# Seven half products instead of eight (Strassen) for the gate and up products of the expert stage

## What is computed

```
scores = softmax(x @ gate_w.T)                     # 64 experts, the best 8 are kept in w_e
flat = w_e[:, inv_map]                             # (tokens, 8 groups, 8)
soft = softmax(where(flat == 0, -1e9, flat))
xg = x[:, None, :] + einsum('ngi,ghi->ngh', soft, mask_up_w)
g = einsum('ngh,gih->ngi', xg, gate_proj_w)
u = einsum('ngh,gih->ngi', xg, up_proj_w)
d = einsum('ngi,ghi->ngh', silu(g) * u, down_proj_w)
y = einsum('ng,ngh->nh', flat.sum(-1), d)
out = layernorm(x + y)
```

## Time and profile before

| | us |
|---|---|
| median of 3 runs | 2915.49 (2913.86 to 2915.83) |
| the profiled execution | 2915.24 |
| its span, first to last instruction | 2913.5 |
| PE busy in it | 2688.2 (92%) |
| DVE, ACT, POOL busy | 1899.0, 1596.0, 1313.3 |

### The profile page before, as it was taken

The page is one execution under the profiler, slowest core; times in us unless marked ns, Lnnn a source line. Parts: engine busy times, 40 slices in busy tenths (PEclk is TensorE's granted clock), DMA queues, the critical chain, the costliest instruction groups (busy, mean ns, idle before and its releaser), DMA issues. The chain is left out here.

```text
span 2913.5 us, 48708 instructions
## 1 busy us (share of the span) xinstructions
PE 2688.2 (92%) x16876; PEld 1534.9 (53%) x16876; DVE 1899.0 (65%) x3477; ACT 1596.0 (55%) x3668; POOL 1313.3 (45%) x1326
## 2 busy tenths in 40 slices
PE   6789886899999999869987999999899999999998
PEld 4667672455555555534435666666554444444443
DVE  5778897887787787677746788886473333332335
ACT  7999993665656656644427777776442222222121
POOL 3889895877676766324325111111042222222121
PEclk8999998999999999989997999999989999999999
DMA  5112113322221222420011000000032211111201
GB/s 166 39 55 77 43 40 84 94 44 41 44 39 37 44 40 60 141 71 1 1 46 49 19 20 14 15 20 19 9 101 69 68 31 69 65 67 31 69 33 69
DMA packets 154010, 148.99 MB, mean 51 GB/s; under 512 B 108721, under 2 KB 113201, under 8 KB 152402
## 3 DMA queue, kind: packets, MB, share of 16 engines
q1 hardware_dynamic: 153810, 146.49, 17.7%
HBM read 112.57 MB, written 4.52 MB: 40 GB/s over the span
## 5 line engine op out<-in xcount | busy, mean ns | idle before, releaser
L2233 POOL TENSOR_TENSOR s_state<-s_state,s_ct 128x512 f32<-128x512 f32 x256 | 326.6, 1301 | 81.0 <-DVE s_state L2408 78.6
L891 POOL TENSOR_TENSOR m_aTl<-m_prod,m_aTh 128x512 bf16<-128x512 f32 x88 | 101.6, 1155 | 559.7 <-ACT m_aTh L965 559.7
L2408 DVE TENSOR_TENSOR_SCAN s_state<-s_decay,s_psd 128x512 f32<-128x512 f32 x256 | 301.7, 1209 | 67.3 <-PE s_psd L2553 33.3
L1150 DVE TENSOR_TENSOR m_prod<-m_bank,m_gated 128x512 f32<-128x512 f32 x88 | 60.9, 692 | 406.3 <-ACT m_gated L963 406.3
L963 ACT ACTIVATE m_gated<-m_bank 128x512 f32<-128x512 f32 x88 | 52.5, 596 | 403.0 <-PE m_bank L1281 220.4
L1264 PE MATMUL m_bank<-m_xTh,m_wh 128*128 128x512 bf16 x704 | 267.4, 380 | 2.0 <-DVE m_prod L1150 1.2
L1265 PE MATMUL m_bank<-m_xTl,m_wh 128*128 128x512 bf16 x704 | 267.2, 380 | 0.0
L2553 PE MATMUL s_psd<-ident,s_v 128*128 128x128 f32 x1024 | 164.7, 286 | 43.0 <-DVE s_state L2408 22.0
L2309 ACT ACTIVATE s_decay<-s_dt,s_nega 128x508 f32<-128x508 f32 x256 | 181.6, 710 | 19.3 <-DVE s_state L2408 19.2
L2322 ACT ACTIVATE s_v<-s_uT,s_bT 128x512 f32<-128x512 f32 x256 | 182.1, 712 | 1.1 <-PE s_psd L2553 1.0
L2553 PEld LDWEIGHTS s_psd<-ident,s_v 128*128 128x128 f32 x1024 | 121.8, 146 | 90.0 <-ACT s_v L2322 47.9
(11 more groups left out here) (511 smaller groups left out, 7866.9 us busy)
## 6 DMA issues: line engine op xcount, KB each, us to landing
s_ct<-ssm_bc SPq DMA_DIRECT2D x64, 256.0 KB, 3.0
m_scale<-moe_scale SPq DMA_DIRECT2D x64, 256.0 KB, 3.1
m_stage<-in_moe_w_dram SPq DMA_DIRECT2D x16, 768.0 KB, 4.6
m_stage<-in_moe_w_dram SPq DMA_DIRECT2D x8, 1024.0 KB, 8.5
X<-in_x_dram SPq DMA_DIRECT2D x4, 1024.0 KB, 11.1
staging<-in_xa_wq_dram SPq DMA_DIRECT2D x8, 512.0 KB, 4.1
a_cf<-in_ctxT_dram SPq DMA_DIRECT2D x16, 256.0 KB, 2.9
staging<-in_xa_wo_dram SPq DMA_DIRECT2D x8, 512.0 KB, 4.4
```

What stands on the lines that cost most here:

```text
L2233: pool.tensor_tensor(h, h, ct[t % 4][:, s * P:(s + 1) * P].unsqueeze(1).broadcast_to([P, KB, P]), ALU.mult).then_inc(weighted, 1)
L2408: dve.tensor_tensor_scan(state[i % RING][:, :], decay[t % 2][:, s, :, :].rearrange("p m t -> p (m t)"), ps_d[i % 2][:, :], 0.0, ALU.mult, ...
```

## The change

In sections 1 to 7 a block's gate and up are made together. The tokens of a quarter are two halves of 256 (`TH`), the 512 inputs two halves, and gate and up are the two halves of the weights; the 2 x 2 x 2 half products are replaced by seven, with sums of input halves (S1 to S4) and differences of weight halves (T1 to T4), after Strassen's scheme in Winograd's form. Section 0 stays as it was. In detail:

- PE, `joint`: seven `half_product`s, each 2 input parts times 3 terms of 256 columns. They go to banks 0 (two, one after the other), 1, 2, 3 (two, added up) and 6. Four soft matmuls of 256 columns follow their products one by one: three with 64-row weights, one with 128-row weights (`change`). The down tiles move to the second and third block of a quarter, inside `joint`.
- DVE, `joint`: seven adds of 256 columns give up and gate in SBUF; `finish` (product and scale) of a block runs between the adds of the next, and now reads up from SBUF. ACT copies the first product out of bank 0 before the second may overwrite it, and makes Silu from SBUF.
- `token_sums`: S1 to S4 in bf16 high and low parts, 14 DVE operations and 4 ACT copies a quarter, spread over the three blocks of the quarter behind it: during section 0, the last quarter's at the start of section 1.
- `w_differences`, `difference_high`, `w_difference_low`: T1 to T4 of the next section, 4 subtractions on POOL, 4 copies on ACT and 4 low parts on POOL (each 128 x 768), from block (2, 0) on. They overwrite `stage`, so the next weights are loaded later: ahead of the section's first block, and only when the differences are through.
- From section 1 on soft_half and mover_rows use bank 7 alone. PE then waits between the halves: the second transposes for ACT's two copies of the first, the second mover product for DVE's subtraction on the first.
- On DVE, `mover_rows` gets one more operation a half (`change`); the last block's `finish` comes after the section loop.

Several buffers of the stage share one allocation now (`early`); this adds no instruction. The core of the diff:

```diff
+        sums = early[:, 0:3 * 2 * 2 * TQ * TH // 2].bitcast(BF16).rearrange("p (i x k t) -> p i x k t", i=3, x=2, k=2)
+        gated = [early[:, 6144 + TW * j:6144 + TW * (j + 1)] for j in range(2)]
+        diff = [fr.sb(f"m_diff{j}", [P, 4, 2, 2, I], BF16, st) for j in range(2)]
+        partial = diff[0][:, :, :, :, :].rearrange("p i x k n -> p (i x k n)")[:, 0:4 * TH].bitcast(F32).rearrange("p (k t) -> p k t", k=2)
...
+        ps_x, ps_v, ps_w, ps_z, ps_y = bank[0], bank[1], bank[2], bank[3], bank[6]
...
+        def later_tiles(c, b):
+
+            return ((), (0, 1), (2, 3))[b] if NB[c] == 3 else ((), (0, 1, 2, 3))[b]
...
+        def mover_bank(c, h):
+            return ps_m[h] if c == 0 else ps_m[1]
...
-                    last_c, last_q, last_b = BLOCKS[n - RING]
-                    if (last_q, last_b) == (2, 1) and last_c + 2 < S:
-                        next_weights(last_c + 2)
+                if (q, b) == (0, 0) and c and c + 1 < S:
+                    next_weights(c + 1)
...
+            def w_differences(c, i):
+
+                b11, b21, b12, b22 = halves(stage)
+                if i == 0:
+                    pool.wait_ge(w_low.sem, w_low.at(c, 2))
+                    pool.tensor_tensor(b11, b12, b11, ALU.subtract).then_inc(differed.sem, 1)
+                    pool.wait_ge(differed.sem, differed.at(c - 1, 1))
+                    pool.tensor_tensor(b12, b22, b12, ALU.subtract).then_inc(differed.sem, 1)
+                else:
+                    pool.wait_ge(differed.sem, differed.at(c - 1, 2))
+                    pool.tensor_tensor(b22, b22, b11, ALU.subtract).then_inc(differed.sem, 1)
+                    pool.wait_ge(differed.sem, differed.at(c - 1, 3))
+                    pool.tensor_tensor(b21, b21, b22, ALU.subtract).then_inc(differed.sem, 1)
...
+                        i = n - number(c, 2, 0)
+                        if i in (0, 1) and c + 1 < S:
+                            w_differences(c + 1, i)
+                        if i in (2, 3) and c + 1 < S:
+                            w_difference_low(c + 1, 1 - j, i - 2)
...
+            def sum_high(q, i):
+                act.wait_ge(summed.sem, summed.at(q, (3, 6, 9, 13)[i]))
+                out = sums[:, i, 0, :, q * TH:(q + 1) * TH] if i < 3 else xTh[:, LOW_ROWS, tokens(q, 1)]
+                act.activation(out, partial[:, :, :], ACT.Copy).then_inc(summed_high.sem, 1)
...
+            def joint(c, q, b):
+                n = number(c, q, b)
+                k = mixed(n)
+                act.wait_ge(products.sem, products.at(k, 1))
+                act.wait_ge(a_low.sem, a_low.at(n - 2))
+                act.activation(prod[n % 2][:, FIRST_HALF], ps_x[:, 0:TH], ACT.Copy).then_inc(x_read.sem, 1)
+                if k:
+                    a_high_part(*BLOCKS[n - 1])
+                act.wait_ge(joined.sem, joined.at(k, 6))
+                act.activation(gated[n % 2][:, :], gated[n % 2][:, :], ACT.Silu).then_inc(gated_done.sem, 1)
...
+            def finish(n):
+                dve.wait_ge(gated_done.sem, gated_done.at(n))
+                dve.wait_ge(joined.sem, joined.at(mixed(n)))
+                dve.tensor_tensor(prod[n % 2][:, :], prod[n % 2][:, :], gated[n % 2][:, :], ALU.mult).then_inc(raw_done.sem, 1)
+                weighted(n)
...
+            def joint(c, q, b):
+                n = number(c, q, b)
+                k = mixed(n)
+                first, second = prod[n % 2][:, FIRST_HALF], prod[n % 2][:, SECOND_HALF]
+                gate_one, gate_two = gated[n % 2][:, FIRST_HALF], gated[n % 2][:, SECOND_HALF]
+                tiles = later_tiles(c, b)
+                def add(out, a, b, after, product):
+                    dve.wait_ge(products.sem, products.at(k, product))
+                    if after:
+                        dve.wait_ge(joined.sem, joined.at(k, after))
+                    dve.tensor_tensor(out, a[:, 0:TH], b, ALU.add).then_inc(joined.sem, 1)
+                dve.wait_ge(x_read.sem, x_read.at(k))
+                dve.wait_ge(a_low.sem, a_low.at(n - 2))
+                add(second, ps_z, first, 0, 2)
+                dve.wait_ge(raw_done.sem, raw_done.at(n - 2))
+                add(gate_two, ps_w, second, 1, 3)
+                if k:
+                    finish(n - 1)
+                add(gate_one, ps_x, first, 0, 5)
+                add(first, ps_v, second, 3, 4)
+                add(second, ps_v, gate_two, 4, 4)
+                for t in tiles[:len(tiles) // 2]:
+                    add_tile(*tile_of(c, q, t))
+                add(gate_two, ps_z, gate_two, 5, 6)
+                add(first, ps_y, first, 4, 7)
+                for t in tiles[len(tiles) // 2:]:
+                    add_tile(*tile_of(c, q, t))
...
+                if i == 0:
+                    sum_step(q, 0, t, a21[0], a22[0], ALU.add, ())
+                    sum_step(q, 1, t, t, a21[1], ALU.add, ())
+                    sum_step(q, 2, t, t, a22[1], ALU.add, ())
+                    sum_step(q, 3, sums[:, 0, 1, :, here], t, sums[:, 0, 0, :, here], ALU.subtract, (high,))
+                elif i == 1:
+                    sum_step(q, 4, t, t, a11[0], ALU.subtract, ())
+                    sum_step(q, 5, t, t, a11[1], ALU.subtract, ())
+                    dve.wait_ge(*high)
+                    dve.tensor_tensor(sums[:, 1, 1, :, here], t, sums[:, 1, 0, :, here], ALU.subtract).then_inc(summed.sem, 1)
...
+                        step = n - NB[0]
+                        if 0 <= step < 3 * TQ:
+                            for i in ((0, 1), (2,), (3,))[step % 3]:
+                                token_sums(step // 3, i)
...
+            finish(len(BLOCKS) - 1)
...
+                    pe.wait_ge(softT_ready.sem, softT_ready.at(c, 2 * h))
...
+                    if c and h:
+                        pe.wait_ge(move_low.sem, move_low.at(c, 1))
...
+            def half_product(out, w, x, start, stop):
+                for k in range(2):
+                    for a, b in ((0, 0), (0, 1), (1, 0)):
+                        mm = pe.matmul(out, w[a][:, k, :], x[b][:, k, :], start=start and k + a + b == 0, stop=stop and k == 1 and a == 1)
+                return mm
+            def joint(c, q, b, j):
+                n = number(c, q, b)
+                k = mixed(n)
+                cols = slice(b * P, (b + 1) * P)
...
+                tiles = later_tiles(c, b)
+                def soft(out, h, tok):
+                    return pe.matmul(out, move[j][rows(h), cols], softT[j][rows(h), tok], start=False, stop=True)
+                def free(part):
+                    if k:
+                        pe.wait_ge(joined.sem, joined.at(k - 1, part))
+                if k == 0:
+                    pe.wait_ge(raw_done.sem, raw_done.at(n - 1))
+                free(3)
+                half_product(x, b11, a11, True, True).then_inc(products.sem, 1)
+                if b == 0 and q == 0:
+                    pe.wait_ge(diff_low.sem, diff_low.at(c - 1))
+                if b == 0 and c == 1:
+                    pe.wait_ge(summed.sem, summed.at(q))
+                free(6)
+                half_product(z, t2, s2, True, True).then_inc(products.sem, 1)
+                free(2)
+                half_product(w, t3, s3, True, False)
+                if q in (0, 2) and b == 0:
+                    pe.wait_ge(move_pair.sem, move_pair.at(c - 1))
+                    pe.wait_ge(softT_ready.sem, softT_ready.at(c, q + 2))
+                soft(w, 1, two).then_inc(products.sem, 1)
+                free(5)
+                half_product(v, t1, s1, True, True).then_inc(products.sem, 1)
+                pe.wait_ge(x_read.sem, x_read.at(k))
+                half_product(x, b21, a12, True, False)
+                soft(x, 0, one).then_inc(products.sem, 1)
+                pe.wait_ge(joined.sem, joined.at(k, 1))
+                half_product(z, t4, a22, True, False)
+                pe.matmul(z, change[j][:, cols], softT[j][:, two], start=False, stop=True).then_inc(products.sem, 1)
+                for t in tiles[:len(tiles) // 2]:
+                    down_tile(*tile_of(c, q, t), j if q else 1 - j)
+                free(7)
+                half_product(y, b22, s4, True, False)
+                soft(y, 1, one).then_inc(products.sem, 1)
+                for t in tiles[len(tiles) // 2:]:
+                    down_tile(*tile_of(c, q, t), j if q else 1 - j)
```

More of the change, by code:

```diff
@@ L777, in stage_moe @@
         pick_ready = fr.sem("m_pickready")
+        PLAIN = TQ * NB[0]
+        products = Count(fr, "m_products", 7)
+        joined = Count(fr, "m_joined", 7)
+        x_read = Count(fr, "m_xread")
+        move_pair = Count(fr, "m_movepair", 2)
+        summed = Count(fr, "m_summed", 14)
+        summed_high = Count(fr, "m_summedhigh", 4)
+        differed = Count(fr, "m_differed", 4)
+        diff_high = Count(fr, "m_diffhigh", 4)
+        diff_low = Count(fr, "m_difflow", 4)
         RT_A = 2
```

172 lines of the change are left out of this document (125 added, 47 removed).

## The result

The changed kernel took **3002.82 us** (median of four runs, 2993.76 to 3008.92) beside 2915.39 for the kernel before on the same chip: a ratio of 1.0298, 95% interval 1.0272 to 1.0325. The forecast was 2992, range 2942 to 3032. The profiled execution after took 2993.76, 78.5 more than that of before.

What follows compares the result with a forecast made beforehand. TensorE (PE) was taken to bound the kernel, busy 92% of the span. Terms 9 + 18.5 + 9 + 6 + 5 + 4 + 10 + 9 + 6 = +76.5 on 2915.24 gave 2992 us, range 2942 to 3032.

Steps and rivals of the forecast that it cites:

- PE's queue: Blocks of sections 1 to 7: 5.62 us for 5.49, half products 0.60 less, lone soft terms 0.72 more; 76 blocks +9 us.
- a lone load hides: Rival: a lone 64-row weight load hides under running matmuls, a block takes 5.0 us, total 2946; chance 0.14.
- soft_half: Bank 7 alone: second eight transposes wait for ScalarE's two copies, 2.7 us six times and 2.3 in section 0, 18.5.
- mover_rows: Second mover product waits until the first is copied and subtracted: 5 x 1.35 + 2 x 1.1 = 9 us.
- behind mover: VectorE's mover steps end 3 us into a block without tiles, adds 3 and 6 late: 7 x 0.9 = 6 us.
- The steady block: Sections 1 to 7: VectorE's adds come in time, the sixth by 0.2 us, so PE loses 0.
- Section 0: Token sums meet POOL's long operations: a tile, soft copies and mover subtraction come late; +10 us (3 to 20).
- the forced 1.35: Mover_rows' wait between its two products: copy 0.48, subtraction 0.55, with three semaphore steps 1.35 us.
- Start of section 1: PE drains into bank 0 (1.6); last quarter's sums make copies of x late: +9 us (4 to 14).
- The norm and the end: Last section: ln.vector delays two first blocks, 2 us each, +4; last products behind tile adds and norm, +5.
- Clock: PE falls to 1.2 GHz after long idles, each costing about 1.6 us; four falls of ten idles, +6 (2 to 16).
- Not slower: Rival: loads hide, PE's queue gains 37 us, only forced waits (32.5) and no backlog: 2911; chance 0.08.

## Why the prediction was right, and where it was not

- **PE's queue.** Right in mechanism and price: three lone switches of 0.20 us a block, none hidden, 5.64 us for 5.62. Taking them away gave 35 us and showed it. The rival "a lone load hides" fell: 228 entries of "issue" where the earlier trace rows has 42 and 32, none hidden.
- **soft_half, mover_rows, behind mover.** Right: 2.76 for 2.7, 1.33 and 1.09 for 1.35 and 1.1; 0.92 for 0.9, but in four sections only. One round trip of soft_half in the changed kernel, timeline of PE and ScalarE:

```profile
2440.64 0.63 PE L1422 MATMUL m_bank<-identb,m_soft 128*64 128x128 bf16 x8
2441.14 0.63 ACT L1057 ACTIVATE m_early<-m_early 128x512 f32<-128x512 f32 x1 [1.29 <-DVE m_early L1283]
2441.68 2.04 ACT L1013 ACTIVATE m_softT<-m_bank 64x1024 bf16<-64x1024 bf16 x2
...
2443.86 1.03 PE L1422 MATMUL m_bank<-identb,m_soft 128*64 128x128 bf16 x8 [2.59 <-ACT m_softT L1013]
```

Silu, copies, transposes stand in the order and at the distances of the prediction's walk. One wait behind soft_half the walk left out: in the section of two blocks ScalarE's list has a high part of the next weights ahead of the next copy of x. Timeline of ScalarE and PE there:

```profile
2539.93 1.91 ACT L993 ACTIVATE m_wh<-m_stage 128x2048 bf16<-128x2048 f32 x1
2541.75 0.37 ACT L1053 ACTIVATE m_prod<-m_bank 128x256 f32<-128x256 f32 x1
2542.17 0.28 PE L1496 MATMUL m_bank<-m_xTh,m_wh 128*128 128x256 bf16 x1 [1.31 <-ACT m_prod L1053]
```

- **The steady block.** Right: VectorE in time, the sixth add with 0.14 us to spare where the walk had 0.2, as the extra adds showed. What the walk did not say is that this room is also what stops a better version: with 5.04 us a block VectorE is the later one.
- **Section 0: the sum right, a step wrong.** The mover's subtraction was put 5 us late because of the sums and GpSimd. It was 4.7 late, but without any sums it still was 2.4 beyond the forced 1.35: the copies of differences ahead of it in ScalarE's list, which the prediction listed in the diff and did not put into that queue. Its collision was right. Timeline of GpSimd and VectorE there:

```profile
2204.38 4.52 POOL L911 TENSOR_TENSOR m_wl<-m_stage,m_wh 128x2048 bf16<-128x2048 f32 x1
2205.66 3.78 DVE L1336 TENSOR_TENSOR m_xTl<-m_diff,m_xTh 128x512 bf16<-128x512 f32 x1 [0.70 <-ACT m_xTh L1035]
```

  A 0.69 us subtraction lasted 3.78, until 0.5 behind GpSimd's end. The Trainium skill (SBUF — State Buffer, SBUF: two separate sides) says that a VectorE operation with two SBUF inputs and a GpSimd one that reads SBUF exclude each other for a whole instruction; this row agrees.
- **Start of section 1.** Right: 9.2 for 9, and the run without sums took all but 1.58 of it away.
- **The norm and the end.** Both right: the norm costs 2.05 a time for 2, add 1 late first and the later adds passing it on, as forecast; the last tiles come 7.46 later for 7.5, and the cause was shown by moving one product.
- **Clock.** Mis-sized: +10.5 for +6. The price of a fall was right, 1.6 us (12.9 over eight stretches); the number was not. The prediction took the lower level to follow 2.68 us of idle and let four of ten idles fall to it; eight fell, four of the six at soft_half and all four longer ones.
- **The median.** It lies 11 us above the forecast. 5 of them are the stage (81.7 for 76.5), and the clock is most of these. The other 6 were not in the profiled execution; where the other three spent them no run shows.
- **The sign.** "Not slower" asked for no backlog and hidden loads; neither held as the kernel stood. Both can be brought about, by 128-row weights and another order, and then the kernel is level with before to 0.14% better: the arithmetic's gain is real on PE's queue, and small beside what the other engines must do for it.

## What to carry to other kernels

Cost a cheaper algorithm by the queue of the engine that binds, switches included, and then walk the other engines' lists in order: here seven eighths of the columns made a block longer, because three small matmuls changed the row mode. Weights of 64 rows between 128-row ones are better padded with zeros. When a buffer goes to new work, look who shared it and how far apart the two halves of a round trip can be put, and let a step that another engine waits for stand ahead of side work in every list.

## What was not expected of the hardware

The same idle time before the same work had two outcomes. soft_half's second transposes followed 2.59 us of idle six times; in four sections they ran at 1.2 GHz, eight in 1.03 us, in two at 2.4 GHz, eight in 0.61:

```profile
2336.26 0.61 PE L1422 MATMUL m_bank<-identb,m_soft 128*64 128x128 bf16 x8 [2.59 <-ACT m_softT L1013]
```

What decided between them the runs do not show. And zero rows cost nothing on PE: with 64 of 128 weight rows zero, a soft matmul's distance to the next was 0.11 us, where with 64 rows it was 0.21.
